# Routing of all sequences ahead of sequence 0's own stages in an eight-sequence Mamba, expert and attention kernel

## What is computed

```python
xn = layernorm(x)
x = x + mamba(xn) + moe(xn)
xn = layernorm(x)
x = x + window_attention(xn) + gated_ffn(xn)
```

## Time and profile before

| | us |
|---|---|
| median of three runs | 1018.65 (1018.41 to 1019.23) |
| profiled execution, its own time | 1021.74 |
| its span | 1019.9 |
| PE busy | 810.4 (79%) |
| DVE busy | 760.9 (75%) |
| ACT busy | 638.1 (63%) |
| POOL busy | 434.0 (43%) |

### The profile page before, as it was taken

How to read it: one execution, slowest core, us unless ns; L and a number is a source line. 1 busy time by engine, 2 the same in 40 slices (tenths; PEclk the granted TensorE clock), 3 DMA queues, 4 the chain that set the end, 5 groups by cost and what they waited for, 6 DMA issues and landing times.

```text
span 1019.9 us, 15614 instructions
## 1 busy us (share of the span) xinstructions
PE 810.4 (79%) x5226; PEld 560.0 (55%) x5226; DVE 760.9 (75%) x1059; ACT 638.1 (63%) x1976; POOL 434.0 (43%) x248
## 2 busy tenths in 40 slices
PE   1855788776788788988898799889888986899785
PEld 0622787664554565556555656565556554556443
DVE  7769443445867897789778977897888888786475
ACT  0233566644579566956795689568956884595554
POOL 2368331104564156516742573266426632571100
PEclk9957899998789888999999989999999998899898
DMA  6564799775434254235414541464145414550000
GB/s 218 172 193 137 233 280 299 225 203 132 119 79 98 60 143 99 64 103 145 115 46 120 149 99 41 119 152 106 32 123 148 106 41 124 129 122 15 19 11 12
DMA packets 85952, 123.20 MB, mean 121 GB/s; under 512 B 8560, under 2 KB 43760, under 8 KB 85744
## 3 DMA queue, kind: packets, MB, share of 16 engines
q1 hardware_dynamic: 79584, 115.38, 41.6%
q0 software_dynamic: 6288, 6.82, 3.0%
HBM read 106.21 MB, written 12.29 MB: 116 GB/s over the span
## 4 chain that ended last, share of the span: by engine, by line
PE 36%; DVE 24%; ACT 14%; issue 12%; POOL 8%; DMA 3%; SPq 1%; DVEq 0%; POOLq 0%; ACTq 0%
DVE hst L818 9%; PE more L1446 6%; ACT pexp L1118 5%; PE y_bank L1314 5%; DVE dBu L810 5%; POOL xs_d L1184 3%; ACT dA L1040 3%; POOL hc L1216 3%; ACT pT L1131 2%; PE work L1333 1%; PE work_l L1458 1%; PE work L1359 1%; PE work L1496 1%; PE work_l L1428 1%; PE work L1292 1%
## 5 line engine op out<-in xcount | busy, mean ns | idle before, releaser
L1216 POOL TENSOR_TENSOR hc<-hst,bcr 128x1024 f32<-128x1024 f32 x116 | 273.7, 2360 | 423.1 <-DVE dBu L810 401.6
L818 DVE TENSOR_TENSOR_SCAN hst<-dA,dBu 128x1024 f32<-128x1024 f32 x128 | 291.8, 2280 | 1.9 <-ACT dA L1040 0.9
L1040 ACT ACTIVATE dA<-dt,neg_a 128x511 f32<-128x511 f32 x256 | 171.0, 726 | 34.0 <-DVE hst L818 31.4
L810 DVE TENSOR_TENSOR dBu<-dtu,bcr 128x1024 f32<-128x1024 f32 x128 | 160.4, 1253 | 11.9 <-DMA bcr<-bc_d 1.5
L1314 PE MATMUL y_bank<-pk,hc 128*128 128x128 f32 x1024 | 153.9, 299 | 14.5 <-POOL hc L1216 10.9
L1314 PEld LDWEIGHTS y_bank<-pk,hc 128*128 128x128 f32 x1024 | 128.8, 154 | 50.8 <-issue 23.3
L1446 PE MATMUL more<-pk,pexp 128*96 128x128 f32 x480 | 109.4, 301 | 48.5 <-ACT pexp L1118 43.0
L1446 PEld LDWEIGHTS more<-pk,pexp 128*96 128x96 f32 x480 | 58.1, 129 | 95.4 <-issue 51.9
L1118 ACT ACTIVATE pexp<-work,nmax 128x96 f32<-128x96 f32 x240 | 77.9, 337 | 30.8 <-DVE nmax L965 30.7
L1131 ACT COPY pT<-more 96x512 f32<-96x512 f32 x120 | 69.9, 582 | 36.8 <-PE more L1446 36.3
L965 DVE TENSOR_REDUCE nmax<-work 128x4 f32<-128x384 f32 x60 | 33.4, 557 | 78.3 <-PE work L1367 57.5
(11 more groups left out here) (363 smaller groups left out, 1524.7 us busy)
## 6 DMA issues: line engine op xcount, KB each, us to landing
bcr<-bc_d SPq DMA_DIRECT2D x128, 512.0 KB, 5.1
qbd<-in_wx SPq DMA_DIRECT2D x8, 578.0 KB, 4.6
o_all<-in_wx SPq DMA_DIRECT2D x8, 578.0 KB, 4.8
pT<-in_wx SPq DMA_DIRECT2D x8, 578.0 KB, 5.1
kT<-in_wx SPq DMA_DIRECT2D x8, 578.0 KB, 5.1
vw<-in_wx SPq DMA_DIRECT2D x8, 578.0 KB, 5.0
xs_d<-rbuf POOLq DMA_DIRECT2D x1, 2560.0 KB, 9.7
hst<-in_hidden SPq DMA_DIRECT2D x8, 256.0 KB, 6.6
```

The source lines that it names most:

```text
L810: v.tensor_tensor(dBu[:], dtu[par], bcr[n % RING][:, 0:1, :].to_broadcast([P, NH, L]), ALU.mult).then_inc(s_dBu, 1)
L818: v.tensor_tensor_scan(hst[n % 2][:].rearrange("p h t -> p (h t)"), dA[n % 2][:].rearrange("p h t -> p (h t)"), dBu[:].rearrange("p h t -> ...
L1040: s.activation(dA[n % 2][:, h, 1:L], dt[par][:, h, 1:L], ACT.Exp, scale=neg_a[:, h, n:n + 1]).then_inc(s_dA, 1)
L1216: g_.tensor_tensor(hc[n % 2][:], hst[n % 2][:], bcr[n % RING][:, 1:2, :].to_broadcast([P, NH, L]), ALU.mult).then_inc(s_hc, 1)
```

## The change

The units `stats`, `norm`, `xT`, `gate`, then four constants, `pick`, `count`, `place`, the other constants, and the first three of eight `scatter` units (four indirect DMAs each) now form LEAD, and all engines run LEAD before turn -1. Scatter 3 stands in slot 8 of turn -1 and scatters 4 to 7 in slot 9. The wait for CONSTS moves to the first user. `x_load` of sequences 2 and 3 is issued before `pk`. The zero fill of `xs_d` reads a zeroed `dA` buffer, later than before in POOL's stream (before the last rstd), and the scatters wait for it. MOE_AT becomes 3.

```diff
-MOE_AT = 4
+MOE_AT = 3
-LEAD = [("stats", 0), ("stats", 1), ("norm", 0), ("stats", 2), ("norm", 1)]
+ROUTE_CONSTS = 12
+def lead():
+    out = [("stats", 0)]
+    for k in range(B):
+        if k + 1 < B:
+            out.append(("stats", k + 1))
+        out += [("norm", k), ("xT", k)]
+        if k > 0:
+            out.append(("gate", k - 1))
+    out += [("gate", B - 1), ("route_consts", 0), ("pick", 0), ("count", 0), ("place", 0), ("consts", 0)]
+    return out + [("scatter", k) for k in range(3)]
...
-    put(-1, 14, ("scatter", 0))
+    put(-1, 8, ("scatter", 3))
+    put(-1, 9, *[("scatter", k) for k in range(4, B)])
...
-            x_load(0)
-            x_load(1)
+            for k in range(4):
+                x_load(k)
             sp.dma_start(pk[:], pack).then_inc(s_pack, 16)
-            x_load(2)
-            x_load(3)
-            sp.dma_start(ffn_i, ffn_d).then_inc(s_ffn, 16)
...
                 if name == "norm":
                     sp.wait_ge(s_axn, (k + 1) * NT)
-                    sp.dma_start(seq(xn_d, k), xna[k]).then_inc(s_xast[k], 16)
                     if k + 4 < B:
                         x_load(k + 4)
-                    if k == 0:
+                    sp.dma_start(seq(xn_d, k), xna[k]).then_inc(s_xast[k], 16)
+                    if k == 4:
+                        sp.dma_start(ffn_i, ffn_d).then_inc(s_ffn, 16)
                         sp.wait_ge(s_xast[0], 16)
                         sp.dma_start(x_in[:], seq(xn_d, 0)).then_inc(s_xin, 16)
...
+            def route_consts():
+                dve.wait_ge(s_pack, 16)
+                v.tensor_copy(belowb[:], pc("below")).then_inc(s_const, 1)
+                v.tensor_tensor(gate_row[:], pc("gate_b"), pc("expert_b"), ALU.add).then_inc(s_const, 1)
...
             def pick():
                 dve.wait_ge(s_agate, B)
-                dve.wait_ge(s_zero, 16)
+                dve.wait_ge(s_constp, 1)
+                dve.wait_ge(s_const, ROUTE_CONSTS)
...
             def zero_slots():
-                pool.wait_ge(s_constp, 1)
+                pool.wait_ge(s_const, 8)
                 pool.dma_start(xs_d.rearrange("i j p d -> (i j p d)").rearrange("(q r n) -> q r n", q=P, n=L),
-                               rbuf[:, 0:1, :].to_broadcast([P, NM * H // L, L])).then_inc(s_zero, 16)
+                               dA[1][:, 0:1, :].to_broadcast([P, NM * H // L, L])).then_inc(s_zero, 16)
...
             pe.wait_ge(s_pack, 16)
-            pe.wait_ge(s_const, CONSTS)
...
                     if b == 0:
+                        pe.wait_ge(s_const, CONSTS)
                         pe.wait_ge(s_cbias, 9)
```

More of the change, by code:

```diff
@@ L160 @@
 LAST = last_turn()
-LEAD = [("stats", 0), ("stats", 1), ("norm", 0), ("stats", 2), ("norm", 1)]
+ROUTE_CONSTS = 12
[9 more added lines that the diff above has]
+    return out + [("scatter", k) for k in range(3)]
+LEAD = lead()
 def early():
@@ L691, in norm_of @@
                                     ALU.subtract, ALU.mult).then_inc(s_axn, 1)
[L692 to L722, removed]
@@ new lines, in consts @@
+            def consts():
+                rest = dc[:, 0, 0:I]
+                v.memset(conv_rows[:], 0.0).then_inc(s_cbias, 1)
+                v.tensor_scalar(rest, pc("conv_b"), 0.5, None, ALU.mult).then_inc(s_cbias, 1)
+                for k in range(3):
+                    q = slice(32 * k, 32 * k + 1)
+                    dve.wait_ge(s_cbias, 2 + 3 * k)
+                    v.tensor_copy(conv_rows[q, :], rest[q, :]).then_inc(s_cbias, 1)
+                    if k < 2:
+                        v.tensor_copy(conv_part[:], rest).then_inc(s_cbias, 1)
+                        dve.wait_ge(s_cbias, 4 + 3 * k)
+                        v.tensor_tensor(rest, rest, conv_part[:], ALU.subtract).then_inc(s_cbias, 1)
+                v.tensor_copy(identb[:], pc("ident")).then_inc(s_const, 1)
+                v.tensor_copy(bandb[:], pc("band").rearrange("p (v k) -> p v k", v=3).unsqueeze(2)
+                              .to_broadcast([P, 3, RG, KW])).then_inc(s_const, 1)
+                for h in range(NH):
+                    v.tensor_scalar(diag_d[:, h, :], pc("ident"), pc("d")[:, h:h + 1], None, ALU.mult).then_inc(s_const, 1)
+                v.tensor_scalar(q_scale[:], pc("heads"), float(HD) ** -0.5, None, ALU.mult).then_inc(s_const, 1)
+                v.tensor_scalar(q_bias[:], pc("heads"), pc("bq"), float(HD) ** -0.5, ALU.mult, ALU.mult).then_inc(s_const, 1)
+                dve.wait_ge(s_expa, 1)
+                v.tensor_scalar(neg_a[:], exp_a[:].rearrange("p (h n) -> p h n", h=NH), -1.0, None, ALU.mult).then_inc(s_const, 1)
+                dve.wait_ge(s_ffn, 16)
+                v.tensor_scalar(ffn[:], ffn_i, 1.0 / 127.0, None, ALU.mult).then_inc(s_const, 1)
+                dve.wait_ge(s_const, FFN_CONSTS - 1)
+                v.tensor_scalar(ffn[:, 0, :], ffn[:, 0, :], 0.5, None, ALU.mult).then_inc(s_const, 1)
+                dve.wait_ge(s_const, FFN_CONSTS)
@@ L802, in early @@
                             v.tensor_tensor(bias_rest[:], bias_rest[:], bias_part[:], ALU.subtract).then_inc(s_bias, 1)
+            for name, k in LEAD:
+                early(name, k)
             def times_b(n, b, par):
@@ L1032, in early @@
                     last.then_inc(s_mr, 1)
+            for name, k in LEAD:
+                early(name, k)
             def decays(n, b, par):
+                if b == 0 and n == 0:
+                    act.wait_ge(s_const, CONSTS)
+                if b == 0 and n == 1:
+                    act.wait_ge(s_zero, 16)
                 if n == 0:
@@ L1182, in early @@
                     pool.wait_ge(s_route, ROUTE_SLOTS)
-                    for t in range(TT):
+                    pool.wait_ge(s_zero, 16)
+                    for t in range(k * NT, k * NT + NT):
                         g_.indirect_dma_start(xs_d.rearrange("i j p d -> (i j p) d"),
@@ L1188, in _ @@
                 early(name, k)
-            pool.wait_ge(s_const, CONSTS)
             def rows(j, b):
@@ L1234, in body @@
                     elif name == "ss":
+                        if b == 0:
+                            pool.wait_ge(s_const, CONSTS)
                         pool.wait_ge(s_ss, b * 6 + 6)
```

21 lines of the change are left out of this document (14 added, 7 removed).

## The result

| | before | after |
|---|---|---|
| median, us | 1018.62 (1018.41 to 1019.23, 4 runs) | 1031.87 (1029.77 to 1034.49, 4 runs) |
| ratio | | 1.0111, 95% interval 1.0082 to 1.0141 |
| profiled execution, own time | 1021.74 | 1033.07 |
| its span | 1019.9 | 1031.3 |
| last expert add (start) | 234.62 | 247.97 |

The account below looks back on a forecast made before the run. Routing and POOL's scatter bound up to 105, then the 40 expert tiles; what counts is when the first expert transpose runs. +10.4 for its start, +1.25 and +1.0 among the tiles give +12.6 on the median 1018.65: 1031.3 us, range 1022 to 1036.

Parts of the forecast that it names:

- The lead: Norms, transposes and gates ahead of the routing: PE at the lower clock, 0.22 a weight load, last gate at 33.7.
- Constants: DVE's other constants, 4.9, now lie between routing and sequence 0's convolution, which waits for them: 49.7.
- Sequence 0's stages, alone: Sequence 0's convolutions, projections and the way to its scan: 44.3 in sum, first scan at 94.0 instead of 74.66.
- The scatter: POOL's scatter DMAs start at 43.5 and end at about 101, about as before, because sixteen wait behind `xdn`.
- The start of the experts: First expert transpose on PE stands behind `hs1` of sequence 1, tokens in by then: 115.4 instead of 105.0, +10.4.
- Among the tiles: MOE_AT = 3 puts one more scan step among the expert tiles, +1.25, and uncovers `xdbl`, +1.0: together +2.2.
- To the end: After 235 the turns follow in fixed order, so a shift there was expected to reach the end unchanged.
- The first: Rival: PE's clock rises in the lead, which ends 6.4 earlier: +6.2, 1024.9; chance 0.24.
- The second: Rival: PE's clock is up nearly everywhere, also in convolutions, projections and `hs1` of sequence 1: -2.1, 1016.5; chance 0.08.
- The third: Rival: the scatter sets the start of the experts and is earlier, PE starting at 98: -4.8, 1013.9; chance 0.07.
- The fourth: Rival: `pk` or the fill lands 4 to 5 late, and PE or the scatter slips as much: 1036; chance 0.09.

Follow-up runs that it names:

- e7: The change again, unaltered, in another series: 1032.17 us, 1.0130 of the kernel before.
- e2: The change with 36 wide bf16 matmuls, their results unused, on PE ahead of `pk`: 1032.27 us, 1.0110 of the kernel before.
- e1: The change with all constants on DVE ahead of the routing instead of behind it: 1023.66 us, 1.0031 of the kernel before.
- e5: The change with all 32 scatter DMAs behind `xdn`, none in the lead: 1037.99 us, 1.0179 of the kernel before.
- e3: The kernel before with only MOE_AT = 3: 1019.08 us, 0.9994 of the kernel before.
- e9: The change with 36 wide matmuls ahead of `pk` and four more behind each sequence's gates: 1030.75 us, 1.0121 of the kernel before.
- e10: The change with constants ahead of the routing, two scatter units in the lead, tokens loaded a slot earlier, MOE_AT = 3: 1016.63 us, 0.9994 of before.
- e11: e10 plus 36 wide matmuls ahead of the lead, four behind each sequence's gates but the last, feed-forward constants behind placing: 1015.71 us, 0.9977 of the kernel before.
- e6: The change with MOE_AT = 2 instead of 3: 1036.29 us, 1.0159 of the kernel before.
- e8: The change with constants ahead of the routing, two scatter units in the lead, tokens loaded a slot earlier, MOE_AT = 2: 1018.21 us, 0.9993 of before.

## Why the prediction was right

Forecast 1031.3 and slower, measured 1031.87. The direction and the path up to `hs1` of sequence 1 were right. That the total was met within 0.6 us is in part luck: errors of 0.4 to 1.6 cancelled on the way, and the last add, forecast 12.6 later, came 13.35 later in one execution and 10.72 in the other. Step by step:

| step | predicted | after |
|---|---|---|
| weight load in the lead | 0.22 | 0.22 |
| last gate ends | 33.7 | 32.7 |
| scatters start | 43.5 | 42.50 |
| first convolution matmul | 49.7 | 48.92 |
| stages of sequence 0 | 44.3 | 44.2 |
| first scan | 94.0 | 93.16 |
| first scan to `hs1` of sequence 1 | 14.7 | 14.7 |
| last scatter landed | 101 | issued at 94.31 |
| first expert transpose | 115.4 (+10.4) | 115.83 (+10.8); e7 114.79 (+9.8) |
| from there to the last add | +2.25 | +2.5; e7 +0.9 |
| last add | 247 | 247.97; e7 245.34 |

- *The lead.* The choice that decided was the clock, and it was right: with no wide work ahead, transposes and gates stayed at 1.2 GHz (0.22 a load). What I read from the earlier trace rows, that they can hold the full clock once it is there, was wrong beyond a short stretch: in e2 they lost it within the second sequence. The eighth norm by my own figures ends at 25.3 (8.39 + 7 x 2.41), not 24.9; it ended at 24.3, under PE's work either way. PE's first transposes (12.64) waited for `pk`, 0.6 more than taken, and the pitch was 2.45 instead of 2.65.
- *Constants.* 4.9 was taken and DVE spent 43.79 to 48.9 on them. Of the time from 16.43 to 21.76 some 0.7 belonged to constants that moved ahead, not 0.4, so the rest took 0.4 longer here than before. What I didn't see is that the 6.89 us in which DVE waits for the gates would hold them all. e1 shows that this is the largest part of the loss, 8 us of the median.
- *Sequence 0's stages, alone.* 44.3 against 44.2, with errors that cancel. The terms as listed add up to 44.7; the 0.4 for the bias was left out of the sum. The first convolution took 6.38 (6.0 taken), the second 3.60 (4.0), and from the end of `xdbl` to the next matmul it was 4.8 (5.5).
- *The scatter.* The end was put 5 too late, since 1.45 a DMA came from the earlier trace rows, with its landing and its hitches. Undisturbed the pitch was 1.27. Single issues of 1.8 and more come only where the scatter lies beside scan steps (before from 78.29 on, e5 from 96.21 on); in the change all but the last issues were over by the first scan. It changed nothing, as the scatter had about 11 us to spare (last one issued at 94.31, tokens asked for at 107.95, some 2 of it the landing), and e5 shows the same.
- *The start of the experts.* Right in time and half right in mechanism. That PE reaches the transpose by way of `u` of sequence 1 and `hs1` was right, to 0.1. That PE would not wait for the tokens was **wrong**: it waited 1.63 (2.44 in e7). `hs1` began 0.8 earlier than forecast and was 0.4 quicker, 6.31 with its bias instead of 6.7, because the clock rose in it (its last load took 0.19, the one before 0.34). These 1.2 hid most of the wait. I had named the load's place behind slot 3's `bc_rows` and priced it at nothing: I had counted when the scatter would be over, and not that SP issues the load only at 107.95, behind a 512 KB load.
- *Among the tiles.* +2.25 lies between the two executions' +2.5 and +0.9. e3, the kernel before with only MOE_AT changed, gives +2.5, 0.4 of it from a later start. The size is thus not confirmed to better than 2.6. Left out was a gain: directly behind `hs1` the first tile ran at the full clock. From its transpose to its first `down` it was 3.1 instead of 4.3.
- *To the end.* A shift at the last add was found again at the end to about 4 us either way, no better. I had expected it unchanged.

The rivals. The first (clock up in the lead, 1024.9) did not happen by itself. e9 made it happen, with fillers in the lead: the routing started 3.5 earlier (6.4 in the rival) and the last add came 4.4 to 7.0 earlier (6.2), but the total is only 1.4 below e7's. The second had the clock up everywhere and fell with it. The third, the intended effect, needs `hs1` of sequence 1 to be over by 98: it was over at 114. e10 and e11 come nearest, with `hs1` from 96.70 to 103.0 in e10, and there the experts do start before 105. The fourth (a late pack) was not seen, 12.64 instead of 12.0.

## What to carry to other kernels

Before a step is moved off a chain to the front, ask what will stand in its place behind it: here the routing came 13 us earlier, and one sequence's stages, each of which waits for the one before and which had run free in the routing's shadow, came 18.5 later and then set the start of the experts. Then look for the wait that the new order creates (DVE's 6.89 behind the gates) and put into it what would otherwise lie behind. And judge an earlier start of a long phase by its end: twice a start 6 to 7 us earlier was given back (e6, and e8 beside e10). What had been done ahead of the phase now lay in it; how the 6 to 7 us divide between that work and the lower clock of the first tile was not measured.

## What was not expected of the hardware

- The 256 KB load of tokens took 7.3 to 8.2 us from issue in the nine profiled executions in which a 512 KB load was issued 0.7 to 1.0 ahead of it (7.84 in the change), and 2.7 to 3.0 in the four (before, e3, e5, e8) in which the last one was 5.6 or more ahead. The median 512 KB load lands in 5.3, so the figures are about what the two take one behind the other (an estimate: 5.3 + 2.8, less the 0.7 between the issues, is 7.4).
- Transposes and eight-column gates behind wide bf16 matmuls were at 2.4 GHz for one sequence and at 1.2 GHz from the second on (e2); four wide matmuls between sequences kept them at 2.4 GHz (e9).
- The granted clock is recorded as 1.00 over a lead whose loads show 1.2 GHz. The window view of the changed kernel, in the columns of the earlier trace rows:

```profile
12.00:33.00 21.00, 20.10 (x96) 19.77 (x96) 13.54 (x71) 5.00 (x9) 6.31 (x6) 1.00 0.92 300
...
45.00:94.00 49.00, 27.59 (x81) 16.10 (x82) 18.91 (x36) 11.27 (x16) 31.85 (x32) 0.78 0.40 131
```

  96 loads in 19.77 are 0.21 each. Early in a program, go by the duration of a known instruction rather than by PEclk.
- The kernel before varies more than its first three runs showed: 25 runs of one series went from 1013.4 to 1027.6. The mean granted clock goes with it, from 0.916 in the fastest to 0.900 in the slowest; what moves the clock is open. The twelve runs of e11 still left an interval of 0.25% to either side.
